# Convolution-style attention block on one core: GpSimd's gating operations spread over 25 units in place of 21

## The reference

```python
xn = silu(group_norm(x, gn_scale, gn_offset))       # 32 groups of 16 channels
q, k, v = split(einsum('bxyc,cd->bxyd', xn, w_qkv), 3)    # 8 heads of 64
sim = einsum('bhdi,bhdj->bhij', q * 64 ** -0.5, k)
out = einsum('bhij,bhdj->bhid', softmax(sim), v)
return einsum('bxyd,dc->bxyc', out, w_out) + b_out + x
```

## Time and profile before

| | |
|---|---|
| median of three executions | 3614.14 us (3612.40 to 3614.34) |
| the profiled execution, its own time | 3612.53 us |
| its span, first to last instruction | 3610.7 us |
| granted TensorE clock, mean | 0.994 |
| busy: PE, DVE, ACT, POOL | 98%, 81%, 76%, 67% of the span |
| the first image's exponentials start at | 91.1 us |

### The profile page before, as it was taken

One profiled execution on the slowest core, in us unless ns is written; L12 is line 12 of the kernel. 1 busy time (PEld: TensorE's weight loads), 2 busy tenths in 40 slices (PEclk: granted clock), 3 DMA queues, 4 the chain that ended last, 5 costly groups with the idle time before them and its releaser, 6 DMA issues.

```text
span 3610.7 us, 91300 instructions
## 1 busy us (share of the span) xinstructions
PE 3536.5 (98%) x31822; PEld 2074.1 (57%) x31822; DVE 2932.3 (81%) x3762; ACT 2738.8 (76%) x3075; POOL 2424.0 (67%) x2238
## 2 busy tenths in 40 slices
PE   6999999999999999999999999999999999999998
PEld 3555555555555556555555555555555565555554
DVE  7787888878888787887878888787887878887777
ACT  3887877878777787777878778787787877878776
POOL 1594866849577494775948659495684957749455
PEclk8999999999999999999999999999999999999999
DMA  3213313233222323223233132332323222232232
GB/s 97 71 36 96 68 41 94 53 82 65 58 77 52 82 64 71 65 59 93 48 83 80 37 94 47 91 68 42 93 53 82 65 64 71 55 86 59 50 86 45
DMA packets 178014, 245.82 MB, mean 68 GB/s; under 512 B 53536, under 2 KB 86304, under 8 KB 177568
## 3 DMA queue, kind: packets, MB, share of 16 engines
q1 hardware_dynamic: 177568, 239.94, 28.1%
HBM read 88.35 MB, written 33.82 MB: 34 GB/s over the span
## 4 chain that ended last, share of the span: by engine, by line
PE 89%; DVE 5%; issue 3%; ACT 2%; POOL 1%; DMA 0%; DVEq 0%; SPq 0%; ACTq 0%; POOLq 0%
PE SD L1140 33%; PE PV L1282 18%; PE TP L1155 11%; PE ST L1252 11%; PE ST L1253 11%; PE ST L1223 2%; PE ST L1216 1%; DVE mx L912 1%; DVE Pl L942 1%; ACT Ph L744 1%; DVE st L919 1%; PE SD L1205 0%; ACT QK L698 0%; DVE QK L858 0%; PE PV L1140 0%
## 5 line engine op out<-in xcount | busy, mean ns | idle before, releaser
L627 POOL TENSOR_TENSOR Pl<-P,Ph 128x512 f16<-128x512 f32 x1024 | 1319.0, 1288 | 1098.6 <-ACT Ph L744 1098.3
L741 ACT ACTIVATE P<-ST,cns 128x1024 f32<-128x1024 f32 x1024 | 1141.7, 1115 | 789.9 <-PE ST L1253 727.9
L912 DVE TENSOR_REDUCE mx<-TP 128x1 f32<-128x1024 f32 x1024 | 1246.2, 1217 | 211.6 <-PE TP L1155 206.7
L744 ACT ACTIVATE Ph<-ST,cns 128x1024 f16<-128x1024 f32 x1024 | 1134.5, 1108 | 0.0
L942 DVE TENSOR_TENSOR Pl<-P,Ph 128x512 f16<-128x512 f32 x1024 | 1029.7, 1006 | 29.8 <-ACT Ph L744 25.1
L1282 PE MATMUL PV<-V,Ph 128*128 128x129 f16 (+2 forms) x10240 | 859.5, 210 | 9.4 <-ACT Ph L744 2.6
L1282 PEld LDWEIGHTS PV<-V,Ph 128*128 128x128 f16 x10240 | 769.6, 97 | 134.5 <-issue 8.8
L1282 PE MATMUL PV<-V,Pl 128*128 128x65 f16 x8192 | 832.2, 192 | 0.0
L1282 PEld LDWEIGHTS PV<-V,Pl 128*128 128x128 f16 x8192 | 721.2, 98 | 109.5
L1252 PE MATMUL ST<-QK 128*128 128x512 f16 x2048 | 776.3, 379 | 3.2 <-DMA QK<-shift_rows 2.2
L1253 PE MATMUL ST<-QK 128*128 128x512 f16 x2048 | 776.6, 379 | 0.0
(11 more groups left out here) (129 smaller groups left out, 2864.4 us busy)
## 6 DMA issues: line engine op xcount, KB each, us to landing
QK<-QK SPq DMA_DIRECT2D x384, 256.0 KB, 4.9
x_in<-in_x SPq DMA_DIRECT2D x61, 512.0 KB, 3.6
res<-in_x SPq DMA_DIRECT2D x120, 256.0 KB, 4.4
out<-res SPq DMA_DIRECT2D x120, 256.0 KB, 3.5
V<-V SPq DMA_DIRECT2D x16, 1040.0 KB, 6.3
QK<-shift_rows SPq DMA_DIRECT2D x256, 64.0 KB, 3.5
shift_rows<-ms SPq DMA_DIRECT2D x256, 1.0 KB, 3.2
V<-in_L_conv_w_qkv SPq DMA_DIRECT2D x4, 768.0 KB, 10.7
```

Of the source, the lines that this page charges most:

```text
L627: nc.gpsimd.tensor_tensor(Pl[:, v % 4, HALF:], P32[:, v % 2, HALF:], Ph[:, v % 4, HALF:], ALU.subtract).then_inc(lo_pool, 1)
L741: nc.scalar.activation(P32[:, v % 2, :], ST[:, slot, :], ACT.Exp, scale=cns[:, 0:1])
L744: nc.scalar.activation(Ph[:, v % 4, :], ST[:, slot, :], ACT.Exp, scale=cns[:, 0:1]).then_inc(exp_done, 1)
L912: nc.vector.reduce_max(mx[:, hh, qb:qb + 1], TP[:], AX.X).then_inc(top_drained, 1)
```

## The change

The 32 gating operations of an image are dealt out half by half. The 16 of the first half take 13 units from (1,9) on and end in (2,5); the 16 of the second half take the 12 units from (2,6) to (3,1), one, one and two at a time: each half up to the unit before the one in which its first job stands. By unit, from (1,9): 1, 1, 1, 1, 2, 1, 1, 1, 2, 1, 1, 1, 2, and then 1, 1, 2 four times. ACT's z and tanh are moved along: a tanh stands one unit before its piece's first operation, as it did. Nothing else is changed.

```diff
-Z_AT = [(1, 8), (1, 10), (1, 13), (1, 15), (2, 2), (2, 5), (2, 7), (2, 10)]
-TANH_AT = [(1, 9), (1, 11), (1, 14), (2, 0), (2, 3), (2, 6), (2, 8), (2, 11)]
-SILU_FROM = (1, 10)
+Z_AT = [(1, 7), (1, 11), (1, 14), (2, 1), (2, 4), (2, 7), (2, 10), (2, 13)]
+TANH_AT = [(1, 8), (1, 12), (1, 15), (2, 2), (2, 5), (2, 8), (2, 11), (2, 14)]
+SILU_FROM, SILU_UNITS = (1, 9), (13, 12)
...
     n = 16 * step + u - 16 * SILU_FROM[0] - SILU_FROM[1]
-    first = 3 * (n // 2) + 2 * (n % 2)
-    return [divmod(k, 4) for k in range(first, first + 2 - n % 2) if 0 <= k < 4 * PIECES]
+    half = n >= SILU_UNITS[0]
+    n, units = n - SILU_UNITS[0] * half, SILU_UNITS[half]
+    ops = 4 * PIECES // 2
+    if not 0 <= n < units:
+        return []
+    return [divmod(k + ops * half, 4) for k in range(ops * n // units, ops * (n + 1) // units)]
```

## The result

The changed kernel takes 3622.93 us (median of ten executions, 3620.57 to 3624.56), the kernel before 3613.82 us (ten, 3612.16 to 3614.36): a ratio of 1.0026, 95% interval 1.0017 to 1.0035. It is slower by 9.1 us, more than the 0.2% that counts as a change here. On the chip of a later group of runs the same kernel, unedited, gave 1.0027 (1.0016 to 1.0039). The profiled execution is the shortest of the ten, 3620.57 us with a span of 3618.8; it shows 8.1 of the 9.1 us. The chain of waits of this profile is followed back over 8% of the span only, so it is not used. The lines of the changed kernel stand 5 higher behind the edit: L627 is L632, L610 is L615, L912 is L917, L1140 is L1145, L1155 is L1160.

A forecast was written before the change was run, and what follows sets the result against it. The prediction took TensorE's (PE's) pace as the bound. Steady images -5.4, start -2.4 and the wait at (3,2) +3.8 summed to -4.0 us: 3610.1 us against the median of 3614.14, range 3602 to 3623.

The forecast's parts named there:

- z in (1,7): ACT's earliest z, in unit (1,7): costs nothing, covered by 0.88 us idle; without that cover at most 0.8 us per image.
- The job of (2,6): PE's job needing the first half's gating: safe, operands after 4.0 us against 5.4 available, so 0 cost.
- The new wait at (3,2): PE's job needing the second half's gating: operands at 25.1 us against 25.16, costing 0.25 us per image, 3.8 in all.
- The start: Image 0, 160 to 215 us: PE's two waits for POOL vanish, gaining 2.4 us, bounds 0 and 5.2.
- gain (a): Steady images 1 to 13: all 13 PE waits for DVE's maximum vanish, gaining 5.4 us, bounds 0 and 5.4.
- The prediction's own sign of being wrong: In PE's waits between 300 and 3165 us: as many for DVE's maximum (L912) as before, which was 13.
- the rule: DVE's two-input subtraction and POOL's SBUF reads block each other, the later in full; 25 units expose four more subtractions per image.
- DVE stays late: Rival, chance 0.12: the old wait for the maximum remains and another like it comes, 0.41 us per image; 3617 us.
- the other fifteen activations: ACT's z and tanh apart from the z in (1,7): lie further apart than before and cost nothing more.
- late gating: Rival, chance 0.13: gating ends late for the job of (3,2), deciding from 1.0 us per image; at 1.16, 3623.7 us.
- All gain, no cost: Rival, chance 0.29: fewer holds end the wait at (3,2); 3606.3 us, or 3603.5 with all the start's waits gone.
- A wait at the maximum and one at (3,2) don't add: Rival "Nothing": PE's loss at a maximum behind (2,10) is not waited again at (3,2); 3611.7 us, inside the forecast's range.

The follow-up runs named there:

- e1: The changed kernel with the bias additions of (3,0) and (3,2) moved to (3,3) and (3,4): 3618.08 us, ratio 1.0017.
- e12: The changed kernel with POOL's first gating operation of piece 4 in (2,7) in place of (2,6), ACT untouched: 3619.88 us, ratio 1.0018.

## Why the prediction was wrong

It said 3610.1 us, "same", in a range of 3602 to 3623. The median of 3622.93 lies at the upper end of the range, but the direction was wrong: the likeliest case was a gain of 4 us, and it became a loss of 9.

**Right.** The kernel runs at PE's pace, and POOL matters only where PE stops: yes. z in (1,7) costs nothing: ACT's idle time at (1,8) fell from 0.88 to 0.19 us, with no stop. The job of (2,6) has 1.4 us of margin: 1.34 in the trace (the operands are complete at 652.84, the job starts at 654.18). The new wait at (3,2), put at 0.25 us per image and 3.8 us in all, is 0.30, and moving the bias brought 3.5. That the size fits so well is in part luck: the gating ended 25.75 us behind the exponentials of (2,10) and not 25.1 (695.79 against 668.93 + 1.11 = 670.04), above all since the normalisation takes 1.06 in place of 0.61 where DVE holds POOL and the bias 1.77 in place of 1.33; but the stop at (2,15) had moved the job by 0.22 too. The start, put at a gain of 2.4 us, gained 1.8 in one profile and 0.9 in the other.

**Wrong, the first step: gain (a), "I take all 13 waits for the maximum away".** It rested on "DVE meets it less often". POOL's free time did grow: ACT's waits for it fell from 60.9 to 30.4 us, though not to the 20 expected. But DVE's meetings with POOL did not become fewer: 38.5 subtractions per image were held in place of 36.1. And one meeting is enough. At (2,7), 0.05 us between POOL's L605 and DVE's subtraction cost 1.09 us of DVE's time (1.77 against 0.68) and 0.57 of PE's, in each of the 13 images, since the order is written out and repeats itself. The sum should have had 0.57 + 0.22 = 0.79 us per image in place of 0: 10.3 us, where the old waits had cost 5.4 by that sum's own count (about 6.6 with the smaller ones behind them). That is most of the miss. The prediction's own sign of being wrong, as many waits for the maximum as before, came: 13 and 13. I had the mechanism, named it in the sentence on the rule and gave it to the rival "DVE stays late" at 0.12, with 0.41 more per image. That rule was said to expose four more subtractions per image; 2.5 more were held. What was missing was to follow the new positions of POOL's operations against DVE's subtraction unit by unit, as I did for the sum at (3,2). A mean of the load says nothing of an order.

**Wrong, the second step: "the other fifteen activations lie further apart than before; they cost nothing more".** z of piece 3 in (2,1) stands ahead of the drain of the job of that unit and costs 0.49 us in the even images, by itself: it stays when POOL's gating is short and goes when that z is moved. Their spacing was looked at, not what stands behind each on ACT's queue.

**Of the rivals,** late gating was the mechanism at (3,2) in its own size, far from the 1.0 us at which it would decide. "All gain, no cost" fell with gain (a). "A wait at the maximum and one at (3,2) don't add" held in part: e1 shows the other stops unchanged when (3,2) goes, e12 shows (3,2) at 0.24 in place of 0.30 when a larger stop stands before it.

**Open.** Whether 25 units for the gating are better than 21 was not separated from where ACT's activations stand: the version that wins has both the wide schedule and new places, and the old schedule with such places was not run. Why only even images stop at (2,2) was not tested. They are the ones whose (2,0) begins a new pass of the loop, with a stop of 0.3 us at (1,15) in both kernels; image 14, which is even but whose (2,0) begins no pass, has neither stop, which points at the loop and doesn't prove it. The start's and the tail's changes differ from kernel to kernel by up to 3 us, about 1 us of it between two executions of the same kernel, and have not been explained.

## What to carry to other kernels

In a schedule written out by hand, spreading an engine's work lowers its load but also sets a new order against the engine with which it shares a path, and that order is repeated in every pass; write down, for each unit, which of the two starts first, before taking a gain from a lower load. Moving one or two operations by a unit or a few brought 2.5 to 4.7 us here in five runs, by the medians, and nothing in two: it counts when it changes who comes first or takes something out of a queue ahead of what TensorE waits for. Gains of single edits need not add where two of them end the same stop. A releaser named by the profile is only the one that ended last before the wait; a run without its work tells whether it was.

## What the runs showed of the hardware

The hold between DVE's subtraction and a POOL instruction is for the whole instruction in both directions, as the Trainium skill, SBUF — State Buffer, "Who interferes with whom", has it, and the trace agrees: every one of the changed kernel's 591 subtractions over 0.75 us ends 0.54 or 0.55 us behind the end of the POOL instruction that was running when it started (as 653.91 + 1.27 and 653.96 + 1.77; 900.17 + 1.27 and 900.65 + 1.34; 902.14 + 1.27 and 902.37 + 1.59), whenever in it the subtraction had started, and so do all 562 of the kernel before. The other way round, L605 takes 1.80 us in place of 1.27 where the subtraction starts 0.01 us ahead of it. I had not expected that a lead of 0.05 to 0.06 us would repeat, as it did in (2,6) of all thirteen images, where DVE's subtraction took 1.75 to 1.77 us each time. Nor that POOL's gating costs PE so little even at its full: with three quarters of its columns taken away, the kernel before gains 14.0 of 3613.3 us. My estimate is that a better order of the gating could win about as much at most; the best one here wins 6.3.
